# An attention and mixture-of-experts layer: three steps of the attention half in another order

## Chip, cores and metric

The kernel runs on one core of one Trainium2 chip. The metric is the device time of one execution in microseconds (us). The kernel before takes 368.56 us, the median of three runs (367.84 to 369.81).

## What is computed

```python
x = x + attention(layernorm(x), ctx, pos, pos, Wq, Wkv, Wout, bout)   # x: 16 x 128 x 256, ctx: 16 x 128 x 128
x = x + experts(layernorm(x), gate_w, w_gate_up, w_down, ws_gate_up, ws_down)

def attention(x, ctx, pos_map, ctx_pos_map, Wq, Wkv, Wout, bout):     # 32 heads of 8
    q = x @ Wq
    k, v = split(ctx @ Wkv)
    q, k = rope(q, pos_map), rope(k, ctx_pos_map)
    w = softmax(einsum('bqhd,bkhd->bhqk', q, k) / sqrt(8))
    return einsum('bhqk,bkhd->bqhd', w, v) @ Wout + bout
```

The second half routes each token to 6 of 32 experts and adds a shared expert. The change does not touch it. It starts when the attention half has ended, at about 210 us of the span.

## The kernel before

Sixteen batches of 128 tokens pass through a pipeline written out by hand. Every engine has a function `period(b)`, called for b = -3 to 17: the first five calls (`n` from -3 to 1) and the last six (12 to 17) are written out, the ten between them run in a loop of two periods a turn. In the period of batch b the kernel does the scores and exponentials of batch b, begins the row maxima of batch b + 1 (`m1`), transposes the keys of b + 2 (`m2`), projects queries and keys of b + 3 (`m3`), normalises b + 4 (`m4`), and finishes batch b - 1 (`o`). Each period has eight steps g = 0 to 7, one for each group of four heads. An engine takes its instructions strictly in the order written here and waits on semaphores; nothing else sets the order.

On TensorE each step begins with the four score products of batch b, keys by queries (`logits_k`, line 624, into banks STB). In odd steps the row maxima collected so far are transposed (`transpose_max`, line 615). Then comes one product of queries by padded keys, whose rows VectorE reduces to maxima (`logits_q`, line 611, into banks SB). Behind these stand, before the change: in step 0 the value projection of b + 1 (`project_v`, line 601, into bank M0), the transposes of x and context of b + 3 (`transpose_xc`, lines 573 and 574, into M1) and the value products of quads 4 to 7 of batch b - 1 (`weigh_values`, line 635, 32 matmuls); in step 1 the query transposes (`transpose_q`, line 589, into M0) and the key projection (line 578); in step 2 the query projection (line 582); in step 3 the output transposes (line 643); in step 4 the value products of quads 0 to 3 of batch b; in step 5 the attention transposes (line 649); in step 6 the key transposes (`transpose_k`, line 596, into M0); in step 7 the output projection of b - 1 (`project_out`, line 655).

M0 serves in turn the value projection, the query transposes and the key transposes; each must be copied out before the next may write: the values by ScalarE (line 410, semaphore `v_ok`), the queries by ScalarE (line 426), the keys by VectorE (`evac_kT`, line 531, semaphore `kT_ok`). ScalarE also computes the exponentials (line 405, one a step, each also waiting until the value products four steps back have read its buffer), and copies context (line 395, `xcT_ok`), queries and keys (line 416), outputs (`evac_OT`, line 442, after the last value product) and attention (line 420, `attnT_ok`, for which the output projection waits). The value copy of b + 1 waits for all value products of b - 1 as well, since they read the same buffer V. GpSimd rotates and splits queries and keys of b + 3 (lines 264 to 291, tile tokst).

SyncE takes the copied keys kT into the padded tile kz with four transfers a batch (line 319) at the beginning of a period, before it sends the maxima (line 326) in steps 1, 3, 5 and 7. The first product of queries by padded keys, in step 3, waits until all four have landed. kz has two buffers, and the one written was read last by the scores of step 7 of the period before; SyncE therefore waits until all exponentials of that batch are done:

```python
                    else:
                        sp.wait_ge(exp_ok, QUADS * b.n)
```

On its own queue ScalarE issues, in the ten looped periods, the weights of the experts for the second half (352 KB each, after steps 1, 4 and 6).

Of the kernel before, what the change touches and what calls it, by code (L numbers as in the profile page):

```python
# [36 lines left out]
QUADS, SLOT = NH // 4, 32  # L37
# [137 lines left out]
def attention(nc, sem, X, identf, st2, ring, ahead, x, ctx_in, pos, wq, wkv, wout, bout):  # L175
    with ExitStack() as es:
# [119 lines left out]
        @block.sync  # L296
        def _(sp):
            sp.dma_start(POS[:, :, :], pos.rearrange("b p a -> p b a")).then_inc(pos_in, 16)
            for c in range(4):
                sp.dma_start(X[:, 4 * c:4 * c + 4, :], xr[:, 4 * c:4 * c + 4, :]).then_inc(x_in[c], 16)  # L300
                if c == 0:
                    sp.dma_start(CT[0][:, :], ctx_in[0]).then_inc(ctx_in_s[0], 16)
                    sp.dma_start(WQ[:, :, :], wq.rearrange("(c p) n -> p c n", p=P)).then_inc(w_in, 16)
                    sp.dma_start(WKV[:, :], wkv).then_inc(w_in, 16)
                    sp.dma_start(WO[:, :, :], wout.rearrange("(c p) n -> p c n", p=P)).then_inc(w_in, 16)
                    sp.dma_start(BO[:, :], bout.rearrange("(a n) -> a n", a=1).broadcast_to([P, D])).then_inc(bo_in, 16)

            def period(b):
                m1, m4 = b + 1, b + 4
                if inside(m1):  # L310


                    if isinstance(b.n, int) and b.n < 1:
                        sp.wait_ge(kz_zero, 2)
                        sp.wait_ge(kT_ok, m1.n + 1)
                    else:
                        sp.wait_ge(exp_ok, QUADS * b.n)
                    for j in range(4):
                        sp.dma_start(kz[m1.par][32 * j:32 * j + 32, j, :, :],
                                     kT[32 * j:32 * j + 32, :, :]).then_inc(kz_in[m1.par], 16)  # L320
                for g in (1, 3, 5, 7):
                    who, half = (b, (g + 3) // 2) if g < 5 else (m1, (g - 5) // 2)
                    if inside(who):
                        k = 4 * who.n + half
                        sp.wait_ge(mxs_ok, k + 1)
                        sp.dma_start(qst[who.par][MAXROW:P:SLOT, 2 * half:2 * half + 2, :],
                                     mxs[half % 2][:, :]).then_inc(mr_in[half % 2], 16)
                    if g == 1 and inside(m4):
                        at_least(sp, xcT_mm, m4.n - 1)
                        sp.wait_ge(consts, 2)  # L330
                        sp.dma_start(CT[m4.par][:, :], ctx_in[m4.n]).then_inc(ctx_in_s[m4.par], 16)
            periods(sp, period)


# [42 lines left out]
        def _(act):  # L377
# [21 lines left out]
            def period(b):  # L399
                m1, m2, m3, m4, o = b + 1, b + 2, b + 3, b + 4, b + -1  # L400
                for g in range(QUADS):
                    if inside(b):
                        act.wait_ge(st_mm, QUADS * b.n + g + 1)
                        at_least(act, pv_mm, QUADS * b.n + g - 3)
                        act.activation(pw[g % 4][:, :], STB[g % 2][:, :], ACT.Exp, scale=SCALE).then_inc(exp_ok, 1)  # L405
                    if g == 0 and inside(m1):
                        at_least(act, v_mm, m1.n + 1)
                        act.wait_ge(consts, 6)
                        at_least(act, pv_mm, QUADS * b.n)
                        act.copy(Vh[m1.par][:, :, :, 0:HD], M0[:, 0:D].rearrange("p (f h d) -> p f h d", f=2, d=HD)).then_inc(v_ok, 1)  # L410
                    if g == 0 and inside(m3):
                        evac_xcT(m3)
                    if g == 2 and inside(m3) and not (isinstance(b.n, int) and b.n == -3):
                        at_least(act, qk_mm, m3.n + 1)
                        at_least(act, rope_ok, m3.n)
# [1 line left out]
                    if g == 5 and inside(o):  # L417
                        act.wait_ge(attnT_mm, o.n + 1)
                        at_least(act, wo_mm, o.n)
                        act.copy(attnT[:, :, :], OB[o.par][:, D:2 * D].rearrange("p (c t) -> p c t", c=DK)).then_inc(attnT_ok, 1)  # L420
                    if g == 0 and inside(o):
                        evac_OT(o)
                    if g == 1 and inside(m1):
                            at_least(act, qstT_mm, m1.n + 1)
                            at_least(act, st_mm, QUADS * b.n)
# [21 lines left out]
        def _(dve):  # L447
# [85 lines left out]
            def period(b):  # L533
                m1, m2, m3, o, o2 = b + 1, b + 2, b + 3, b + -1, b + -2
                for g in range(QUADS):
# [10 lines left out]
                        statistics2(o2)  # L546
                    if g in (3, 4) and inside(o):
                        normalise(o, g - 3)
                    if g == 6 and inside(m2):
                        evac_kT(m2)  # L550
                    if g == 3 and isinstance(b.n, int) and b.n == -3:
                        dve.wait_ge(qk_mm, 1)
# [10 lines left out]
        def _(pe):  # L563
# [96 lines left out]
            def period(b):  # L660
                m1, m2, m3, o = b + 1, b + 2, b + 3, b + -1
                for g in range(QUADS):
# [6 lines left out]
                    who, u = (b, g + 5) if g < 3 else (m1, g - 3)  # L669
                    if inside(who):  # L670
                        logits_q(who, u)
                    if g == 0 and inside(m1):
                        project_v(m1)
                    if g == 0 and inside(m3):
                        transpose_xc(m3)
                    if g == 0 and inside(o):
                        for q in range(4, QUADS):
                            weigh_values(o, q)
                    if g == 4 and inside(b):
                        for q in range(4):  # L680
                            weigh_values(b, q)
# [7 lines left out]
                        transpose_outputs(o)  # L689
                    if g == 5 and inside(o):  # L690
                        transpose_attn(o)
                    if g == 6 and inside(m2):
                        transpose_k(m2)
                    if g == 7 and inside(o):
                        project_out(o)
            periods(pe, period)


# [708 lines left out]
```

## Time and profile before

| what | value |
|---|---|
| median of 3 runs | 368.56 us |
| profiled execution, its own time | 369.8 us |
| its span | 367.8 us |
| TensorE busy | 315.5 us (86%) |
| VectorE busy | 221.8 us (60%) |
| GpSimd busy | 196.3 us (53%) |
| ScalarE busy | 188.2 us (51%) |

The span runs from the first to the last recorded instruction. PE is TensorE's matmuls, PEld its weight loads, DVE VectorE, ACT ScalarE, POOL GpSimd, SP SyncE. In a timeline each row gives start and length in us, engine, line, operation, what is written and read, how many; rows that follow each other in one group are merged. In brackets stands how long the engine had been idle before, and the instruction by which the profile says it was released. A recorded matmul length holds its way through the array, so successive rows overlap: what a group takes in line is the distance from its start to the next group's start.

### The profile page before, as it was taken

Reading aid. Unit: us, or ns where it says so; the run is one execution under the profiler, and the core shown is the slowest. Engines: PE = TensorE matmul, PEld = TensorE weight load, DVE = VectorE, ACT = ScalarE, POOL = GpSimd, SP = SyncE. Lnnn points to the kernel's source line nnn. Section 1 sums busy time; section 2 is a strip of 40 time slices with the busy share of each in tenths; the row PEclk is TensorE's granted clock in tenths of the full one; section 3 lists DMA queues with packets and bytes.
Section 4 is the critical chain, followed back from the end, with each engine's and each line's share of the span. In section 5 each row is a group of like instructions: output and inputs, shape, how many; then the busy total and the mean of one; then the engine's idle time right before and its main releaser. Section 6 shows DMA issues by size and latency. Waiting matters only on the chain. (4 is left out here: it accounts for less than half of the span.)

```text
span 367.8 us, 9525 instructions
## 1 busy us (share of the span) xinstructions
PE 315.5 (86%) x3094; PEld 218.1 (59%) x3094; DVE 221.8 (60%) x621; ACT 188.2 (51%) x389; POOL 196.3 (53%) x285
## 2 busy tenths in 40 slices
PE   0668999999999999999998558889999989999930
PEld 0445777777777777777676324445765764555520
DVE  4466777676777666777777445788549044454520
ACT  4153668767668767668667375271344342233310
POOL 5569876667866667866200181053788411525460
PEclk9996999999999999999999858999999999999985
DMA  6511114454454454543210033203123275953446
GB/s 169 183 37 30 31 25 116 119 149 118 136 138 115 116 148 115 146 132 87 77 46 3 0 115 111 69 0 87 46 84 105 67 219 181 295 136 44 52 50 228
DMA packets 33292, 37.93 MB, mean 103 GB/s; under 512 B 7808, under 2 KB 27568, under 8 KB 33200
## 3 DMA queue, kind: packets, MB, share of 16 engines
q1 hardware_dynamic: 22610, 22.03, 20.6%
q10 hardware_dynamic: 8030, 11.93, 11.7%
q0 software_dynamic: 2624, 3.61, 5.9%
q8 instruction: 16, 0.26, 0.3%
q14 instruction: 12, 0.10, 0.1%
HBM read 26.36 MB, written 8.96 MB: 96 GB/s over the span
## 5 line engine op out<-in xcount | busy, mean ns | idle before, releaser
L405 ACT ACTIVATE pw<-bank 128x512 f32<-128x512 f32 x128 | 78.0, 615 | 53.3 <-PE bank L635 45.1
L496 DVE TENSOR_REDUCE mx<-bank 128x4 f16<-128x512 f32 x128 | 86.2, 684 | 9.6 <-PE bank L611 8.2
L624 PE MATMUL bank<-qst,kz 128*128 128x128 f16 x512 | 50.3, 221 | 0.3 <-ACT pw L405 0.2
L611 PE MATMUL bank<-kz,qst 128*128 128x512 f16 x128 | 49.6, 389 | 0.9 <-DMA kz<-kT 0.9
L624 PEld LDWEIGHTS bank<-qst,kz 128*128 128x128 f16 x512 | 36.0, 98 | 14.6 <-issue 6.8
L943 POOL DMA_INDIRECT acc<-ac,dst x16 | 23.5, 1471 | 35.3 <-ACT ac L1025 23.4
L264 POOL TENSOR_TENSOR t<-qk,RC 128x512 f32<-128x512 f32 x15 | 19.1, 1272 | 40.2 <-ACT qk L416 40.2
L503 DVE COPY mxs<-bank 8x128 f16<-8x128 f16 x64 | 13.4, 210 | 36.4 <-PE bank L615 36.4
L635 PE MATMUL bank<-pw,V 128*32 128x128 f32 x1024 | 34.6, 276 | 0.0
L1245 PE MATMUL mbank<-hT,WSG 128*128 128x512 f16 (+1 forms) x144 | 32.0, 379 | 0.0
L635 PEld LDWEIGHTS bank<-pw,V 128*32 128x32 f32 x1024 | 26.0, 109 | 7.3 <-issue 5.0
L899 POOL TENSOR_TENSOR ac<-ac,sg 128x512 f32<-128x512 f32 (+1 forms) x9 | 11.8, 1323 | 25.7 <-ACT ac L979 25.7
L269 POOL TENSOR_TENSOR t<-qk,RS 128x256 f32<-128x256 f32 x30 | 24.7, 844 | 0.0
L1245 PEld LDWEIGHTS mbank<-hT,WSG 128*128 128x128 f16 (+1 forms) x144 | 15.0, 106 | 15.6 <-ACT ac L979 0.4
L1257 PE MATMUL mbank<-WSD,ac 128*128 128x256 f32 (+1 forms) x96 | 21.7, 382 | 1.9 <-POOL ac L899 1.9
L289 POOL TENSOR_TENSOR tokst<-rot,tokst 128x256 f16<-128x256 f32 x30 | 20.1, 672 | 4.4
L278 POOL TENSOR_TENSOR rot<-t 128x256 f32<-128x256 f32 x30 | 21.1, 726 | 2.1 <-POOL t L269 1.7
L1257 PEld LDWEIGHTS mbank<-WSD,ac 128*128 128x128 f32 (+1 forms) x96 | 17.9, 189 | 5.4 <-POOL ac L899 2.9
L1029 ACT ACTIVATE ac<-mbank 128x176 f32<-128x176 f32 x16 | 5.1, 317 | 29.9 <-PE mbank L1335 29.9
L615 PE MATMUL bank<-identh,mx 128*128 128x128 f16 x64 | 14.4, 225 | 6.8 <-DVE mx L496 5.2
L1335 PE MATMUL mbank<-ring_gu,xbT 128*64 128x352 f32 x112 | 19.1, 461 | 0.7 <-ACT xbT L819 0.7
L582 PE MATMUL bank<-WQ,xcT 128*128 128x256 f32 x64 | 18.2, 411 | 0.0
(192 smaller groups left out, 640.2 us busy)
## 6 DMA issues: line engine op xcount, KB each, us to landing
ring_gu<-in_L_ffn_w_gate_up ACTq DMA_DIRECT2D x20, 352.0 KB
kz<-kT SPq DMA_DIRECT2D x64, 64.0 KB, 2.0
ring_dn<-in_L_ffn_w_down ACTq DMA_DIRECT2D x10, 352.0 KB
ring_gu<-in_L_ffn_w_gate_up SPq DMA_DIRECT2D x8, 352.0 KB
X<-in_x SPq DMA_DIRECT2D x4, 512.0 KB, 8.1
table<-ac SPq DMA_DIRECT2D x8, 256.0 KB, 2.2
acc<-X SPq DMA_DIRECT2D x4, 512.0 KB, 3.7
out<-acc SPq DMA_DIRECT2D x4, 512.0 KB, 5.6
```

The lines of the kernel that those rows point to most:

```text
L264: eng.tensor_tensor(o1, source[:, :].rearrange("p (x a) -> p x a", a=8), rc, ALU.mult)
L269: ins = eng.tensor_tensor(o2[:, :, :, r], pairs[:, :, :, 1 - r], rs, ALU.mult)
L278: eng.tensor_tensor(rot[:, part], t1[:, part], t2[:, part], ALU.add).then_inc(rot_ok[w], 1)
L289: eng.tensor_tensor(tokst[m.par][:, w, :, a:a + HD], r, hi, ALU.subtract)
L405: act.activation(pw[g % 4][:, :], STB[g % 2][:, :], ACT.Exp, scale=SCALE).then_inc(exp_ok, 1)
L496: dve.tensor_reduce(mx[u // 2 % 2][:, u % 2:8:2], SB[u % 2][:, :].rearrange("p (j t) -> p j t", j=4), axis=AX.X, op=ALU.max, negate=True). ...
L611: pe.matmul(SB[u % 2][:, :], qst[m.par][:, u, :], kz[m.par][:, :, u, :], start=True, stop=True).then_inc(s_mm, 1)
L624: ins = pe.matmul(STB[g % 2][:, j * P:j * P + P], kz[m.par][:, j, g, :], qst[m.par][:, g, :], start=True, stop=True)
L635: ins = pe.matmul(OB[m.par][32 * j:32 * j + 32, (g % 4) * P:(g % 4) * P + P], V[m.par][:, a:a + SLOT], pw[g % 4][:, j * P:j * P + P], star ...
L943: pool.indirect_dma_start(acc[:, :], bass.IndirectOffsetOnAxis(ap=dst[0:USED, k:k + 1], axis=0), ys[j][0:USED, :], None, compute_op=ALU.ad ...
L1245: ins = pe.matmul(GU[2 * (i % 2) + w][0:n, :], WSG[:, c, u, w * SHARED + a:w * SHARED + a + n], hT[:, v, c, 512 * k:512 * k + 512], start= ...
L1257: ins = pe.matmul(DN[m % 2][:, 0:D], ac[k % 2][0:n, f, j * P:j * P + P], WSD[0:n, f, :], start=(f == 0), stop=(f == 2))
```

## The change

The order of four engines is rewritten, and one wait is exchanged. No instruction is added or removed.

- Step 0 on TensorE: value products of b - 1 first, then the x and context transposes, then the value projection. ScalarE follows: output copy, context copy, value copy.
- Step 6 on TensorE: the output projection. Step 7: the key transposes. VectorE's key copy moves from step 6 to step 7.
- SyncE's padded-key transfers wait for the key copy (`kT_ok`) in all periods, as they did in the first ones. The copy comes after the key transposes, and these now stand behind the step-7 scores, the last readers of the kz buffer.

```diff
--- before.py
+++ after.py
@@ -314,7 +314,7 @@
                         sp.wait_ge(kz_zero, 2)
                         sp.wait_ge(kT_ok, m1.n + 1)
                     else:
-                        sp.wait_ge(exp_ok, QUADS * b.n)
+                        sp.wait_ge(kT_ok, m1.n + 1)
                     for j in range(4):
                         sp.dma_start(kz[m1.par][32 * j:32 * j + 32, j, :, :],
                                      kT[32 * j:32 * j + 32, :, :]).then_inc(kz_in[m1.par], 16)
@@ -403,13 +403,15 @@
                         act.wait_ge(st_mm, QUADS * b.n + g + 1)
                         at_least(act, pv_mm, QUADS * b.n + g - 3)
                         act.activation(pw[g % 4][:, :], STB[g % 2][:, :], ACT.Exp, scale=SCALE).then_inc(exp_ok, 1)
+                    if g == 0 and inside(o):
+                        evac_OT(o)
+                    if g == 0 and inside(m3):
+                        evac_xcT(m3)
                     if g == 0 and inside(m1):
                         at_least(act, v_mm, m1.n + 1)
                         act.wait_ge(consts, 6)
                         at_least(act, pv_mm, QUADS * b.n)
                         act.copy(Vh[m1.par][:, :, :, 0:HD], M0[:, 0:D].rearrange("p (f h d) -> p f h d", f=2, d=HD)).then_inc(v_ok, 1)
-                    if g == 0 and inside(m3):
-                        evac_xcT(m3)
                     if g == 2 and inside(m3) and not (isinstance(b.n, int) and b.n == -3):
                         at_least(act, qk_mm, m3.n + 1)
                         at_least(act, rope_ok, m3.n)
@@ -418,8 +420,6 @@
                         act.wait_ge(attnT_mm, o.n + 1)
                         at_least(act, wo_mm, o.n)
                         act.copy(attnT[:, :, :], OB[o.par][:, D:2 * D].rearrange("p (c t) -> p c t", c=DK)).then_inc(attnT_ok, 1)
-                    if g == 0 and inside(o):
-                        evac_OT(o)
                     if g == 1 and inside(m1):
                             at_least(act, qstT_mm, m1.n + 1)
                             at_least(act, st_mm, QUADS * b.n)
@@ -546,7 +546,7 @@
                         statistics2(o2)
                     if g in (3, 4) and inside(o):
                         normalise(o, g - 3)
-                    if g == 6 and inside(m2):
+                    if g == 7 and inside(m2):
                         evac_kT(m2)
                     if g == 3 and isinstance(b.n, int) and b.n == -3:
                         dve.wait_ge(qk_mm, 1)
@@ -669,13 +669,13 @@
                     who, u = (b, g + 5) if g < 3 else (m1, g - 3)
                     if inside(who):
                         logits_q(who, u)
-                    if g == 0 and inside(m1):
-                        project_v(m1)
-                    if g == 0 and inside(m3):
-                        transpose_xc(m3)
                     if g == 0 and inside(o):
                         for q in range(4, QUADS):
                             weigh_values(o, q)
+                    if g == 0 and inside(m3):
+                        transpose_xc(m3)
+                    if g == 0 and inside(m1):
+                        project_v(m1)
                     if g == 4 and inside(b):
                         for q in range(4):
                             weigh_values(b, q)
@@ -689,10 +689,10 @@
                         transpose_outputs(o)
                     if g == 5 and inside(o):
                         transpose_attn(o)
-                    if g == 6 and inside(m2):
+                    if g == 6 and inside(o):
+                        project_out(o)
+                    if g == 7 and inside(m2):
                         transpose_k(m2)
-                    if g == 7 and inside(o):
-                        project_out(o)
             periods(pe, period)
 
 
```

TensorE, steps 6 and 7 and the start of the next step 0, in the period of batch 12. L624 are scores, L611 queries by padded keys, L596 key transposes, L615 the maxima's transpose, L655 the output projection. Before:

```order
L611 MATMUL bank<-kz,qst 128x512
L596 MATMUL bank<-identh,tokst 128x128 x8
L624 MATMUL bank<-qst,kz 128x128 x4
L615 MATMUL bank<-identh,mx 128x128
L611 MATMUL bank<-kz,qst 128x512
L655 MATMUL bank<-WO,attnT 128x256 x2
L624 MATMUL bank<-qst,kz 128x128 x4
```

And now:

```order
L611 MATMUL bank<-kz,qst 128x512
L655 MATMUL bank<-WO,attnT 128x256 x2
L624 MATMUL bank<-qst,kz 128x128 x4
L615 MATMUL bank<-identh,mx 128x128
L611 MATMUL bank<-kz,qst 128x512
L596 MATMUL bank<-identh,tokst 128x128 x8
L624 MATMUL bank<-qst,kz 128x128 x4
```

The projection and the key transposes have changed places around the scores and the maxima's transpose of step 7.

ScalarE, from the last exponential of one period to the query copy (L426) of the next, in the period of batch 1. L410 is the value copy (L414 in the changed file), L395 the context copy, L442 the output copy, L405 an exponential. Before:

```order
L405 ACTIVATE pw<-bank 128x512 x4
L410 COPY V<-bank 128x2x16x8
L395 COPY xcT<-bank 128x384
L442 COPY OT<-bank 128x512
L405 ACTIVATE pw<-bank 128x512
L426 COPY qst<-bank 128x1024
```

And now:

```order
L405 ACTIVATE pw<-bank 128x512 x4
L442 COPY OT<-bank 128x512
L395 COPY xcT<-bank 128x384
L414 COPY V<-bank 128x2x16x8
L405 ACTIVATE pw<-bank 128x512
L426 COPY qst<-bank 128x1024
```

The value copy now comes last of the three copies, the output copy first.

## Rows read from the trace of the kernel before

**Rows 1.** Timeline of TensorE, period of batch 7: start, length, line, operation

```profile
108.59 0.39 PE L624 MATMUL bank<-qst,kz 128*128 128x128 f16 x4
...
109.03 0.59 PE L601 MATMUL bank<-WKV,xcT 128*128 128x256 f32 x2
109.46 0.38 PE L573 MATMUL bank<-identf,xn 128*128 128x128 f32 x2
...
109.88 1.08 PE L635 MATMUL bank<-pw,V 128*32 128x128 f32 x32
...
111.18 0.38 PE L611 MATMUL bank<-kz,qst 128*128 128x512 f16 x1
...
114.13 0.38 PE L611 MATMUL bank<-kz,qst 128*128 128x512 f16 x1
...
115.32 1.08 PE L635 MATMUL bank<-pw,V 128*32 128x128 f32 x32
...
117.49 0.61 PE L596 MATMUL bank<-identh,tokst 128*128 128x128 f16 x8
117.94 0.39 PE L624 MATMUL bank<-qst,kz 128*128 128x128 f16 x4
...
118.75 1.03 PE L655 MATMUL bank<-WO,attnT 128*128 128x256 f32 x4
...
119.62 0.39 PE L624 MATMUL bank<-qst,kz 128*128 128x128 f16 x4
```

**Rows 2.** Timeline of ScalarE, the same period

```profile
111.10 0.37 ACT L410 COPY V<-bank 128x256 f32<-128x256 f32 x1
111.37 0.48 ACT L395 COPY xcT<-bank 128x384 f32<-128x384 f32 x1
111.74 0.60 ACT L442 COPY OT<-bank 128x512 f32<-128x512 f32 x1
...
117.33 0.37 ACT L420 COPY attnT<-bank 128x256 f32<-128x256 f32 x1
```

**Rows 3.** Timelines of weight loads (PEld) and ScalarE, same period and batch 14's

```profile
111.59 0.46 PEld L589 LDWEIGHTS bank<-identh,tokst 128*128 128x128 f16 x8 [0.36 <-POOL tokst L291]
...
118.44 0.10 PEld L615 LDWEIGHTS bank<-identh,mx 128*128 128x128 f16 x1 [0.29 <-DVE mx L496]
...
187.21 0.37 ACT L410 COPY V<-bank 128x256 f32<-128x256 f32 x1
...
187.69 0.46 PEld L589 LDWEIGHTS bank<-identh,tokst 128*128 128x128 f16 x8 [0.36 <-issue]
```

**Rows 4.** Timeline of all engines, last output projection of the attention half

```profile
207.19 0.37 ACT L420 COPY attnT<-bank 128x256 f32<-128x256 f32 x1 [2.17 <-PE bank L649]
...
207.61 1.13 PE L655 MATMUL bank<-WO,attnT 128*128 128x256 f32 x4 [0.46 <-ACT attnT L420]
```

**Rows 5.** Timeline of TensorE in batch -1's period, then windows table with granted clock

```profile
30.29 1.06 PE L596 MATMUL bank<-identh,tokst 128*128 128x128 f16 x8
...
31.32 0.10 PEld L615 LDWEIGHTS bank<-identh,mx 128*128 128x128 f16 x1 [0.24 <-DVE mx L496]
...
core 0: us, PE busy (x) PEld busy (x) DVE busy (x) ACT busy (x) POOL busy (x), PEclk, DMA share, GB/s
...
30.00:32.00 2.00, 2.00 (x13) 1.29 (x13) 1.88 (x4) 0.00 (x0) 1.92 (x4) 0.50 0.01 1
```

**Rows 6.** Timeline of weight loads and TensorE, periods of batches 14 and 16

```profile
193.97 0.10 PEld L615 LDWEIGHTS bank<-identh,mx 128*128 128x128 f16 x1 [0.74 <-DVE mx L496]
...
203.29 1.08 PE L635 MATMUL bank<-pw,V 128*32 128x128 f32 x32
```

**Rows 7.** Timelines of VectorE, SyncE and TensorE, then landings of line 319's transfers

```profile
118.30 0.68 DVE L531 COPY kT<-bank 128x1024 f16<-128x1024 f16 x1
...
21.83 2.53 SPq L319 DMA_DIRECT2D kz<-kT  x4
...
25.93 0.59 PE L611 MATMUL bank<-kz,qst 128*128 128x512 f16 x2 [0.91 <-DMA kz<-kT]
...
DMA to landing us min/median/max: 2.0/2.0/3.1
```

## The prediction

> **What bounds the kernel now.** The change touches only the attention half, so I read that half by period. TensorE's timeline first: from the first score product of one batch (step 0, at 108.59 us) to that of the next (119.62) is 11.03 us [rows 1], and the matmuls stand almost shoulder to shoulder. TensorE sets the pace; the other engines cost time only where it waits for them. I call the period's start E and the start of its step-4 value products (115.32, E + 6.73) W. The next period starts at W + 4.30.
>
> Then TensorE's weight loads, for the holes. Two come back in each period. At step 7 the transpose of the maxima waits for the last row maximum: 0.29 us [rows 3]. At step 1 the query transposes (line 589) start their load at 111.59. In line, 0.22 after the score product at 111.18 [rows 1], they would start at 111.40, so 0.2 us is lost. The profile names GpSimd's key and query split as the releaser. The rows speak against it: ScalarE's copy of the values started 0.49 earlier, at 111.10 [rows 2], and at 187.69, where GpSimd is not named, the load again stands 0.48 behind a value copy [rows 3]. Both products use bank M0, so the transposes wait for that copy. The two holes, 0.5 us a period, are all that a new order can win.
>
> **The change, part by part** (the sum is against the profiled execution's own 369.8 us; the median of the runs shown, 368.56, lies 1.2 below, and I move the sum onto it).
>
> *Step 0, value products first.* The 32 value products take 1.01 (109.88 to 110.89 by their place in line), the context and x transposes 0.42, the value projection 0.43 [rows 1]. Their sum is unchanged, so TensorE reaches the query transposes at the same E + 2.81. What matters is when the value copy runs, since it now stands behind the output copy and the context copy on ScalarE. Before, it started 1.22 after the start of the products [rows 1, 2]. Now the products start at E + 0.44, so the output copy starts by E + 1.66. ScalarE's next instruction starts about 0.11 before the recorded end of the one before (V 0.37 long, next start 0.27 later [rows 2]): output copy 0.49, context copy 0.37, value copy at E + 2.52. The value projection, at E + 1.87 and 0.59 long, ends at E + 2.46, just in time. The copy started at E + 2.51 before. The hole stays; bounds -0.2 (if it vanished) and +0.1 (if the late projection holds the copy back); I take +0.02. The earlier exponential of step 0 frees nobody, since its products are due only in step 4.
>
> *Steps 6 and 7, output projection against key transposes.* The projection (0.87 in line, 118.75 to 119.62) now stands where the transposes stood (117.49, W + 2.17; they take 0.45) [rows 1]. It needs the attention copy, which starts at 117.33, W + 2.01 [rows 2]. Where the projection was seen waiting for this copy it started 0.42 after the copy's start, at 207.61, and the group was 1.13 long instead of 1.03 [rows 4, 1]: its load is not hidden. So it starts at W + 2.43 and the step-7 scores at W + 3.30 (load free) or W + 3.40 (load 0.10 in the open). The maxima's transpose is due 0.22 later (117.94 to 118.44 is 0.50, less the hole of 0.29 [rows 1, 3]), at W + 3.51 to 3.61; the maximum lets it go at W + 3.12, so this hole is gone. Behind it 0.31 (118.44 to 118.75) and the key transposes 0.45: the period ends at W + 4.27 to 4.37, against 4.30. **One hole is traded for another**: -0.03 to +0.07. I take +0.07, by the row that shows a waiting projection.
>
> The Trainium skill ("TensorE: Matmul & The Clock Gate", Part 2, "Step-by-step: what each phase is for") says that the array pulls weight loads ahead of matmuls in flight, so that they overlap. By that the load would be free and the term -0.03. Here the operand loaded is the awaited copy itself, and the trace with its 1.13 disagrees. No other number rests on this.
>
> With +0.02 from step 0 this is +0.09 for each of the twelve periods of batches 1 to 12, which hold all moved pieces: **+1.1** (bounds -0.1 and +2.0; with the hole at step 1 gone, -2.5).
>
> *Fill.* In the period of batch -1 the clock is granted at half, 1.2 GHz (0.50 in 30 to 32 us), and the key transposes at 30.29, 1.06 long, lie wholly inside a wait of the maxima's transpose, which ends at 31.32 [rows 5]. In step 7 they lie in the open before batch 0's first scores: 0.85 at this clock, of which about half is won back where the work behind it runs after the rise to full speed. Bounds 0.4 and 0.85: +0.6. In batch 0's period there is no output projection to put in their old place: they leave the shadow of the step-7 hole and add up to their 0.45 [rows 1]; I take +0.4. Together **+1.0**.
>
> *Drain.* In batch 13's period nothing changes in kind. In batch 14's there are no key transposes; the step-7 hole is 0.74 [rows 6], and the projection moved in front of it fills it, less its own wait of about 0.2 and the open load of 0.1: -0.45. In batch 15's the projection stands between the step-7 scores and the last value products, which start at 203.29 [rows 6]. In front of the scores it delays them by its own 0.97 and the 0.2 of its wait, 1.2; three of the four groups of value products (0.25 each) need not wait for the last exponential, and the end moves by about +0.45 (bounds 0 and 1.2). Nothing covers this: copy, transposes and last projection follow one another to the next half. Together **0**.
>
> *The transfers.* The padded keys' four issues waited for the exponentials of the batch before, now for the key copy. Key transposes, 0.61 long, start at W + 3.92; with a maximum of 0.69 in VectorE's way the copy (0.68 [rows 7]) ends by about E + 1.1. From the first issue to the first product that waited for them was 4.10 us (21.83 to 25.93 [rows 7]), so they are there at E + 5.2. They are needed at 114.13, E + 5.54 [rows 1]. Nothing is late as long as a landing stays near 2.0 us; 3.1 us is the longest seen [rows 7]. Behind these issues SyncE has the maxima's transfer of step 1, some 0.4 later than before, wanted only in step 6. VectorE gets the key copy ahead of the x update and one maximum, 0.68 later; that maximum is wanted at E + 2.5 and ready by about E + 2.1. Cost: nothing, with 0.3 us of cover in the first case and 0.4 in the second.
>
> Sum: 1.1 + 1.0 + 0 = +2.1 us, so 371.9 for the profiled execution and **370.7** for the median.
>
> **The rivals.** *No measurable difference (369.4).* The projection's load is hidden after all: -0.03 a period instead of +0.07, the twelve give 0 with the term of step 0, and 1.0 of fill would give 369.6; with the low bound of the fill 369.2; I write 369.4. For it: the terms are small and half the fill is a guess about the clock. Against: the row of 1.13. By the page named above this would be the case.
>
> *Faster (366.1).* The step-7 hole goes and the projection does not wait. The mechanism: ScalarE, relieved in step 0, has the attention copy done by W + 2.17 instead of W + 2.38. Then -0.29 for each of twelve periods, -3.5, and with +1.0 of fill 366.1. It decides at a copy start 0.2 us earlier. Against: that copy follows an exponential that value products of step 4 release, which moves with W, and not with step 0. If the hole at step 1 goes as well, another -2.5 gives 363.6.
>
> *Slower by more (373).* Under the ring's transfers the last of the padded keys lands up to 1.1 us later than 2.0, against 0.3 of cover: up to 0.8 a period. At 0.2 on average over twelve periods, +2.4 on the forecast: 373.1. It decides at a landing above 2.3 us. For it: the longest is 3.1. Against: issues are now about 1 us later, when the weight transfers of step 6 should be over.
>
> **How the numbers follow.** A measurement of this kernel can tell about 0.5%, 1.8 us, from no change, so faster means under 366.7 and slower above 370.4. My forecast of 370.7 gets 0.40, no difference 0.35, faster 0.13, late transfers 0.12. The forecast lies so near the bound that a quarter of its weight falls below it. Slower: three quarters of 0.40 and the 0.12, 0.42. Same: 0.35 and the other quarter, 0.45. Faster 0.13. The range leaves out the deeper half of the faster case and the far end of late transfers: 367.0 to 373.2.
>
> **What would show it.** Right: a period of 11.05 to 11.15 us; the maxima's transpose of step 7 without a wait; line 655's load waiting 0.2 to 0.3 for the attention copy, its group 1.13 long; the query transposes still 0.48 behind the value copy; ScalarE's long idle before step 0's exponential shorter by 0.85; batch 0's first scores up to 0.85 later. Wrong: a period under 11.0, a wait of the step-3 scores for the padded keys, or query transposes that start in line.

## The result, and the profile after

| | before | after |
|---|---|---|
| median of 4 runs | 368.76 us (367.84 to 369.81) | 382.22 us (378.45 to 383.08) |
| profiled execution, its own time | 369.8 us | 381.86 us |
| its span | 367.8 us | 379.8 us |
| first output transposes (line 643) | 48.09 us | 49.07 us |
| end of the attention half (line 1206) | 210.0 us | 220.92 us |
| TensorE busy | 315.5 us | 320.3 us |

The changed kernel takes 1.033 times as long, 95% interval 1.028 to 1.038. Here and below a time is the median of all runs, while ratios and intervals are formed from each kernel's fast runs, those within 1.5% of its fastest, which leaves out half of the runs of experiments 5 and 8, in experiment 6 one run of 645 us, and beside 9 and 10 one run of the kernel before of 1083 us. The prediction was 370.7 us with a range to 373.2: the side was right, the size far off.

The 12.0 us between the two spans can be placed with the start times of line 643 (step 3 of each period). **Fill**: +0.98 up to the first. **The eleven distances from there to batch 12's period**: 127.82 against 121.42, +6.40. Nine of them alternate between 11.52 and 11.57 where 11.03 stood; the first is 11.68 (11.09 before), the second 12.22. **Drain**, the last four and the way to the end of attention: 10.51, 12.07, 10.24, 6.30 against 10.27, 10.09, 9.24, 5.97, +3.55. **Second half**, which the change does not touch: +1.1.

TensorE's timeline of batch 7's period, now from 112.96 (E) to 124.47:

```profile
112.96 0.39 PE L624 MATMUL bank<-qst,kz 128*128 128x128 f16 x4
...
113.49 1.08 PE L635 MATMUL bank<-pw,V 128*32 128x128 f32 x32
114.50 0.44 PE L573 MATMUL bank<-identf,xn 128*128 128x128 f32 x2
114.78 0.27 PE L574 MATMUL bank<-identf,CT 128*128 128x128 f32 x1
114.89 0.60 PE L601 MATMUL bank<-WKV,xcT 128*128 128x256 f32 x2
...
116.42 0.61 PE L589 MATMUL bank<-identh,tokst 128*128 128x128 f16 x8 [0.44 <-ACT V L414]
...
120.12 1.08 PE L635 MATMUL bank<-pw,V 128*32 128x128 f32 x32
...
122.56 1.13 PE L655 MATMUL bank<-WO,attnT 128*128 128x256 f32 x4
123.53 0.39 PE L624 MATMUL bank<-qst,kz 128*128 128x128 f16 x4
123.75 0.22 PE L615 MATMUL bank<-identh,mx 128*128 128x128 f16 x1
123.81 0.38 PE L611 MATMUL bank<-kz,qst 128*128 128x512 f16 x1
124.02 0.61 PE L596 MATMUL bank<-identh,tokst 128*128 128x128 f16 x8
124.47 0.39 PE L624 MATMUL bank<-qst,kz 128*128 128x128 f16 x4
```

ScalarE and the weight loads of the same period:

```profile
114.64 0.58 ACT L442 COPY OT<-bank 128x512 f32<-128x512 f32 x1
115.52 0.48 ACT L395 COPY xcT<-bank 128x384 f32<-128x384 f32 x1 [0.30 <-PE bank L601]
115.89 0.38 ACT L414 COPY V<-bank 128x256 f32<-128x256 f32 x1
...
116.39 0.46 PEld L589 LDWEIGHTS bank<-identh,tokst 128*128 128x128 f16 x8 [0.74 <-POOL tokst L291]
...
122.56 0.73 PEld L655 LDWEIGHTS bank<-WO,attnT 128*128 128x128 f32 x4 [0.43 <-ACT attnT L422]
```

E is the start of the period and W that of its step-4 value products, as in the prediction. Read against [rows 1 to 3]: from E to the step-4 value products it is 7.16 us, where 6.73 stood; from these to the next E 4.35, where 4.30 stood. The loss lies in the first part. The idle time before the query transposes' load has grown from 0.36 to 0.74, and their distance behind E from 3.03 to 3.46. ScalarE's rows above show why: the context copy (L395) starts at 115.52, just behind the end of the value projection (114.89 + 0.60), and in brackets it names that projection. The value copy queued behind it starts at E + 2.93.

In the second part the load of L655 waits 0.43 in step 6, and L615 has no wait any more.

In the drain, the period of batch 14. TensorE's timeline, then line 319's landings and the windows table with the granted clock (PEclk):

```profile
197.26 0.23 PE L615 MATMUL bank<-identh,mx 128*128 128x128 f16 x1 [0.56 <-DVE mx L496]
199.10 0.58 PE L611 MATMUL bank<-kz,qst 128*128 128x512 f16 x1 [1.60 <-issue]
199.47 1.06 PE L643 MATMUL bank<-identf,OT 128*128 128x128 f32 x4
```

```profile
L319 SPq DMA_DIRECT2D kz<-kT x4: 558/588/592, 193.7 to 195.6; - x4
...
DMA to landing us min/median/max: 2.0/2.2/3.4
```

```profile
core 0: us, PE busy (x) PEld busy (x) DVE busy (x) ACT busy (x) POOL busy (x), PEclk, DMA share, GB/s
195.00:198.00 3.00, 1.87 (x22) 1.14 (x19) 2.14 (x5) 2.71 (x5) 0.00 (x0) 1.00 0.36 86
198.00:201.00 3.00, 1.90 (x10) 1.47 (x10) 1.05 (x2) 0.07 (x1) 0.00 (x0) 0.65 0.02 5
201.00:204.00 3.00, 3.00 (x46) 2.12 (x45) 1.73 (x4) 1.37 (x4) 0.00 (x0) 0.78 0.00 0
```

The first product of queries by padded keys started 0.10 behind L615 in this period of the kernel before (189.56, 189.66); here it starts 1.84 behind it, with TensorE idle for 1.60. The last of the four transfers was issued at 195.6 and the slowest landing took 3.4, which gives 199.0. From the first issue (193.70) to the product's place in line (197.36) there are 3.7 us here; in batch 7's period it is 4.9 (issue at 114.03, product at 118.93), since steps 0 to 2 there also hold the x and context transposes and the key and query projections of a batch to come, and the last periods have none of these. Behind this pause and the 0.56 ahead of it the granted clock falls to 0.65, a mix of TensorE's two levels (0.5 is 1.2 GHz): the output transposes take 1.06 where 0.60 is their length at 2.4 GHz.

The odd distance of 12.22, batch 2's period, is a third matter. SyncE's and TensorE's timelines:

```profile
55.46 3.52 SPq L319 DMA_DIRECT2D kz<-kT  x4
59.12 0.58 SPq L326 DMA_DIRECT2D qst<-mxs  x1
...
61.87 0.40 PE L624 MATMUL bank<-qst,kz 128*128 128x128 f16 x4 [0.52 <-DMA qst<-mxs]
```

The four issues took 3.52 instead of 2.46. The maxima's transfer stands behind them in SyncE's queue, 0.9 later than in the other periods, and the scores of step 4 wait for it until 2.75 behind its issue. In the same period ScalarE issued its first weight transfer at 58.73, 0.39 ahead of the maxima's (in batch 7's period it comes 0.64 behind). Experiments 4 and 5 are about such meetings.

### The profile page after: what moved, and what is told of

The parts are those of the page before. It is cut to its first block and busy times, and to the rows that moved or that the text cites. A ratio compares the mean times of both kernels' runs of the same rounds, so it can differ in the third digit from the quotient of the medians.

```text
span 379.8 us, 9525 instructions
## 1 busy us (share of the span) xinstructions
PE 320.3 (84%) x3094; PEld 217.2 (57%) x3094; DVE 222.6 (59%) x621; ACT 192.0 (51%) x389; POOL 196.3 (52%) x285
## 5 line engine op out<-in xcount | busy, mean ns | idle before, releaser
L405 ACT ACTIVATE pw<-bank 128x512 f32<-128x512 f32 x128 | 76.7, 603 | 50.9 <-PE bank L635 30.3
L611 PE MATMUL bank<-kz,qst 128*128 128x512 f16 x128 | 49.8, 391 | 2.2 <-issue 1.8
L624 PE MATMUL bank<-qst,kz 128*128 128x128 f16 x512 | 50.4, 222 | 0.9 <-DMA qst<-mxs 0.5
L624 PEld LDWEIGHTS bank<-qst,kz 128*128 128x128 f16 x512 | 37.5, 99 | 14.6 <-issue 3.4
L1335 PE MATMUL mbank<-ring_gu,xbT 128*64 128x352 f32 x112 | 20.5, 488 | 0.7 <-ACT xbT L819 0.7
L655 PE MATMUL bank<-WO,attnT 128*128 128x256 f32 x64 | 18.1, 405 | 2.2 <-ACT attnT L422 1.0
```

What stands on the lines that cost most here:

```text
L611: pe.matmul(SB[u % 2][:, :], qst[m.par][:, u, :], kz[m.par][:, :, u, :], start=True, stop=True).then_inc(s_mm, 1)
L624: ins = pe.matmul(STB[g % 2][:, j * P:j * P + P], kz[m.par][:, j, g, :], qst[m.par][:, g, :], start=True, stop=True)
L1335: ins = pe.matmul(EB[k % 2][lane, 0:2 * INNER], xbT[:, c, e * CAP:e * CAP + LANE], ring.gu[place][:, e % 2, c, :], start=(c == 0), stop=(c ...
```

## The experiments

All changes are in step 0 unless a diff shows more. A kernel's time stands beside runs of the kernel before on the same chip. A period's length is read as a distance between starts of line 643.

**1. The change, with ScalarE's value copy ahead of the context copy.**

```diff
                         evac_OT(o)
-                    if g == 0 and inside(m3):
-                        evac_xcT(m3)
                     if g == 0 and inside(m1):
...
                         act.copy(Vh[m1.par][:, :, :, 0:HD], M0[:, 0:D].rearrange("p (f h d) -> p f h d", f=2, d=HD)).then_inc(v_ok, 1)
+                    if g == 0 and inside(m3):
+                        evac_xcT(m3)
```

> The changed kernel with one difference on ScalarE: in step 0 the value copy stands before the context copy (output, value, context). Theory 1 (the context copy waits for the value projection, by its guard on v_mm, and holds the value copy behind it): the value copy starts right behind the projection's end, 0.34 earlier, the query transposes 0.4 earlier, periods 11.1 instead of 11.54, about 5 us less: 377. Theory 2 (the late value projection itself holds the value copy, so its place among the copies does not matter): no change, 382.

Measured: 376.68 us beside 369.09, ratio 1.020 (1.011 to 1.029). ScalarE's and TensorE's timelines, batch 7's step 0 and 1:

```profile
114.46 0.37 ACT L412 COPY V<-bank 128x256 f32<-128x256 f32 x1 [0.30 <-PE bank L601]
114.73 0.48 ACT L395 COPY xcT<-bank 128x384 f32<-128x384 f32 x1
...
114.98 0.60 PE L589 MATMUL bank<-identh,tokst 128*128 128x128 f16 x8
```

From batch 4's period on the period is 11.13: 0.41 of the 0.51 is gone with two instructions of ScalarE exchanged. So the context copy's wait made it. What is left, +0.10 over the 11.03 of before, is what the prediction had (+0.09). The two periods ahead of these are longer, 11.97 and 12.05: in each the scores of step 4 wait for the maxima, 0.66 and 0.70 us, and the first weight transfer is issued 0.42 and 0.05 ahead of the maxima's. Batch 14's pause is there too (1.13).

**2. The kernel before with the change's step 0 alone.** Against the changed kernel:

```diff
-                        sp.wait_ge(kT_ok, m1.n + 1)
+                        sp.wait_ge(exp_ok, QUADS * b.n)
...
-                    if g == 7 and inside(m2):
+                    if g == 6 and inside(m2):
                         evac_kT(m2)
...
-                    if g == 6 and inside(o):
-                        project_out(o)
-                    if g == 7 and inside(m2):
+                    if g == 6 and inside(m2):
                         transpose_k(m2)
+                    if g == 7 and inside(o):
+                        project_out(o)
```

> The kernel before with the change's step 0 alone (value products first, value projection last, output copy first on ScalarE); steps 6 and 7 and the transfers' wait as before. Theory 1: period 11.03 + 0.43 = 11.47, 12 to 13 periods, about 374.5. Theory of the prediction (step 0 costs 0.02 a period): 369. If the loss comes from steps 6 and 7 instead: no slower than 369.

Measured: 375.51 us, ratio 1.018 (1.010 to 1.026). Periods 11.46 and 11.51 in turn, +0.46, and no product of any of them waits for a transfer; the drain is as before (10.19, 10.19, 9.23, 5.96), with no late transfer. Its period is 0.06 shorter than the whole change's: that is the size of steps 6 and 7.

**3. The whole change, but step 0 in the old order on TensorE and ScalarE.** TensorE's part, ScalarE's copies likewise:

```diff
+                    if g == 0 and inside(m1):
+                        project_v(m1)
+                    if g == 0 and inside(m3):
+                        transpose_xc(m3)
                     if g == 0 and inside(o):
...
-                    if g == 0 and inside(m3):
-                        transpose_xc(m3)
-                    if g == 0 and inside(m1):
-                        project_v(m1)
```

> The changed kernel with step 0 in its old order on TensorE and ScalarE; output projection in step 6, key transposes in step 7 and the new wait stay. The value projection at the head of step 0 must now wait for the key copy, which ends at E + 1.07: it starts at E + 1.1 instead of 0.44, and its hole of 0.67 is added to 0.07 of the waiting output projection: period 11.75, about 378. Rival (the two halves are independent and step 0 carries all of the loss): 370.

Measured: 383.69 us, ratio 1.039 (1.030 to 1.048), worse than expected. TensorE's timeline:

```profile
116.31 0.70 PE L601 MATMUL bank<-WKV,xcT 128*128 128x256 f32 x2 [0.49 <-DVE kT L531]
```

The value projection at the head of step 0 writes bank M0, which holds the keys until VectorE has copied them; with the key transposes in step 7 it waits 0.49 for that copy, and with its load in the open takes 0.10 longer. The period is 11.85 (batch 3's 12.52, where the scores of step 4 wait 0.50 for the maxima). So the change's two halves belong together: key transposes in step 7 need a step 0 that leaves M0 alone at first.

**4. The change, with the value projection between value products and transposes** (copies: output, values, context). Meant to take away the hole of step 1 altogether.

```diff
                         for q in range(4, QUADS):
                             weigh_values(o, q)
-                    if g == 0 and inside(m3):
-                        transpose_xc(m3)
                     if g == 0 and inside(m1):
                         project_v(m1)
+                    if g == 0 and inside(m3):
+                        transpose_xc(m3)
```

> The changed kernel with the value projection between the value products and the x and context transposes, and the copies in that order (output, value, context). Theory 1: value copy at E + 2.17, query transposes in line at E + 2.8, so the hole of step 1 is gone too: period 11.54 - 0.65 = 10.9, about 374 (the fill, the late keys of batch 14 and the output projection's wait stay). Theory 2: the hole of the kernel before, 0.2, stays: period 11.1, 377.

Measured: 382.19 us, ratio 1.035 (1.027 to 1.043): a miss. The query transposes do follow in line, yet the looped periods are 11.55 to 11.88 from batch 3's on. SyncE's, ScalarE's and TensorE's timelines show a new wait:

```profile
118.53 0.58 SPq L326 DMA_DIRECT2D qst<-mxs  x1
...
118.61 0.39 ACTq L122 DMA_DIRECT2D ring_gu<-in_L_ffn_w_gate_up  x1
...
121.80 0.40 PE L624 MATMUL bank<-qst,kz 128*128 128x128 f16 x4 [0.68 <-DMA qst<-mxs]
```

The maxima of 2 KB are waited for until 3.27 us behind their issue. A weight transfer of 352 KB is issued 0.08 behind them. One further product waited 2.34 for padded keys in an early period, and batch 14's again came late (12.39).

**5. The same, with the first weight transfer issued after step 2 instead of step 1.**

```diff
-                    if g in (1, 4, 6) and not isinstance(b.n, int):
-                        ring.load_first(act, b.n - 2, (1, 4, 6).index(g))
+                    if g in (2, 4, 6) and not isinstance(b.n, int):
+                        ring.load_first(act, b.n - 2, (2, 4, 6).index(g))
```

> The kernel v_second (382) with the first of ScalarE's three weight transfers of a period issued after step 2 instead of step 1. Theory 3: in v_second the maxima's transfer of step 1 is issued at 118.53 on SyncE, in line behind the four padded-key issues, and the 352 KB weight transfer at 118.61 shares the 16 engines with it; its landing takes 3.3 us and step 4 waits 0.7. With the weights 1.3 later it lands in about 2 us: no wait of the step-4 scores, period 10.9, about 372 to 374. Rival (SyncE's late issue alone is the cause, and 3.3 us is what such a small transfer takes): no change, 382.

Measured: 374.16 us in 10 runs beside 369.81 in 25, ratio 1.006 (0.999 to 1.013). Idle time of TensorE's products that the maxima's transfer ended, in the view of waits, of experiment 4 and then of this one (us in total, times, longest):

```profile
PE bank L624 <- DMA qst<-mxs: 5.5, 9, 0.8
```

```profile
PE bank L624 <- DMA qst<-mxs: 1.1, 4, 0.4
```

The periods are 11.14 on average. All nine waits of step 4 are gone, with one issue of another queue moved: the collision of the two transfers is shown. It was not removed but moved. The four waits left are those of the scores of step 6, for the maxima that are sent in step 3, and the weight transfer now stands just ahead of these (batch 6's period: weights issued at 104.95, maxima at 105.20). The ratio went from 1.035 to 1.006, by the medians of all runs to 1.012. Not all of that is this waiting: experiment 4 also lost 2.34 us once to padded keys (0.78 here) and 1.1 us more behind batch 14's pause (distance 10.02 against 8.91). In batch 14's period the padded keys still come late (landing at most 3.1 us, period 11.56).

**6. Experiment 1 with the old order of steps 6 and 7, and the old wait, from batch 12's period on.**

```diff
+                    elif isinstance(b.n, int) and b.n > 12:
+                        sp.wait_ge(exp_ok, QUADS * b.n)
...
-                    if g == 6 and inside(o):
+                    last = isinstance(b.n, int) and b.n >= 12
+                    if g == (7 if last else 6) and inside(o):
                         project_out(o)
```

Key transposes and key copy go back to step 6 in these periods in the same way.

> The kernel act_v_second (376.7) with the old order of steps 6 and 7 and the old wait in the written-out last periods (batch 12 on). Theory 4 (in the short last periods the padded keys, issued 1 us later, have no cover, and the wait of 1 to 1.6 us also drops the clock): no wait in step 3 of batch 14's period and no half clock after it; in batch 15's period the scores of step 7 are early again (-0.4). Together -1.5 to -3: 374 to 375. Rival (that late landing is chance or not tied to the order): the wait stays, 376 to 377.

Measured: 375.81 us, ratio 1.015 (1.004 to 1.026) where experiment 1 had 1.020; the intervals overlap, so the verdict rests on the trace. TensorE's timeline at the place of the 1.60, step 3 of batch 14's period (all lines stand two further down):

```profile
191.42 0.23 PE L617 MATMUL bank<-identh,mx 128*128 128x128 f16 x1 [0.56 <-DVE mx L498]
191.52 0.38 PE L613 MATMUL bank<-kz,qst 128*128 128x512 f16 x1
191.73 0.60 PE L645 MATMUL bank<-identf,OT 128*128 128x128 f32 x4
```

No product of this period waits for padded keys, and none runs at half clock. The transfers, issued from 186.89 on, are 4.6 us ahead of the product instead of 3.7, and all four landed within 2.0: they have their cover back.

**7. The kernel before with step 0 in the order of experiment 4** (steps 6 and 7 untouched).

> The kernel before with step 0 as value products, value projection, transposes of x and context, and the copies output, value, context; steps 6 and 7 and the transfers' wait as before. Theory 1: the value copy starts at E + 2.2 and the query transposes stand in line, so the hole of 0.22 at step 1 goes, and neither the output projection waits nor are the padded keys or the maxima late: period 10.82, 13 periods, about 366. Rival (the hole is GpSimd's, as the profile names it, or the maxima's transfer of step 4 comes late here too): 368.5 or more.

Measured: 369.69 us in 10 runs, ratio 0.997 (0.992 to 1.001). The periods are 10.90 to 10.91, 0.13 less than before: the hole of step 1 was real, but worth 0.13 and not 0.2. That is 1.5 us over eleven distances, about what the measurement can tell; its interval holds 1, so no gain is claimed. The profiled 364.48 us comes mostly from an earlier fill (first line 643 at 44.08 instead of 48.09).

**8. Experiment 7 with the output projection in step 7 moved ahead of the maxima's transpose**, to fill its hole with no swap of steps.

```diff
+                    if g == 7 and inside(o):
+                        project_out(o)
...
-                    if g == 7 and inside(o):
-                        project_out(o)
```

> The kernel f_vsecond with the output projection in step 7 moved from behind the products of that step to between the scores and the maxima's transpose, so that it fills the wait for the last maximum. The attention copy ends 0.4 before it. The hole of 0.29 goes; the copy of the maxima comes 0.6 later and the product of step 0 that overwrites its bank may wait 0.1 to 0.15 for it: period 10.82 - 0.15 to 0.29, about 363 to 364.5. Rival (the later copy and transfer of the maxima cost as much): 366 or more.

Measured: 370.64 us, ratio 0.996 (0.991 to 1.001). Every second period reaches 10.7; the others are 11.35 to 11.66, with this in the timelines of SyncE, ScalarE and TensorE:

```profile
102.52 0.59 SPq L326 DMA_DIRECT2D qst<-mxs  x1
...
102.47 0.39 ACTq L122 DMA_DIRECT2D ring_gu<-in_L_ffn_w_gate_up  x1
...
105.75 0.40 PE L624 MATMUL bank<-qst,kz 128*128 128x128 f16 x4 [0.77 <-DMA qst<-mxs]
```

**9 and 10. Experiments 7 and 8 with the weight transfer after step 2** (diff of experiment 5).

> The kernel before with step 0 in the order value products, value projection, context transposes (ScalarE's copies: output, values, context), and the first weight transfer of a period issued after step 2 instead of after step 1. The order of step 0 alone gave periods of 10.90 us and no wait for the maxima, so there is nothing left for the later weight transfer to repair: theory (the weight transfer hurts only where it meets the maxima's transfer) expects the same 10.90 and the time of f_vsecond, ratio to before 0.994 to 0.998. Rival: a weight transfer issued 1.3 us later collides with the padded keys' transfer that starts behind step 7, and the step-3 scores wait: slower than before by 1 to 3 us.

> g_outfirst (output projection in front of the maxima's transpose) with the first weight transfer issued after step 2. If the wait of the step-4 score maxima for their transfer (0.50 to 0.77 us in every other period) comes from the weight transfer that starts beside it, it goes: all periods at 10.7 us, 12 x 0.33 = 4 us less than the kernel before, ratio 0.987 to 0.992. Rival: the maxima's transfer is late because its maximum is, whatever else moves: periods still alternate and the ratio stays at 0.996.

Measured: 371.82 us, ratio 1.004 (1.001 to 1.007), and 369.81 us, ratio 1.001 (0.997 to 1.005), beside 370.13. Both miss: in 9 the time is the rival's, but not for its reason, since no product of the looped periods waits for padded keys. The distances are 10.9 to 11.5 in 9 and 11.06 on average in 10 (without its first, 11.82, in which a product waited 0.97 for padded keys). ScalarE, SyncE and TensorE in 9, batch 7's period:

```profile
113.73 0.59 ACT L418 COPY qk<-bank 128x512 f32<-128x512 f32 x1 [0.27 <-PE bank L582]
113.90 0.39 ACTq L122 DMA_DIRECT2D ring_gu<-in_L_ffn_w_gate_up  x1
114.24 5.56 SPq L326 DMA_DIRECT2D qst<-mxs  x3
114.45 0.60 ACT L405 ACTIVATE pw<-bank 128x512 f32<-128x512 f32 x1
115.55 0.60 ACT L405 ACTIVATE pw<-bank 128x512 f32<-128x512 f32 x1 [0.49 <-PE bank L635]
...
116.51 0.38 PE L649 MATMUL bank<-identf,attn 128*128 128x128 f32 x2
116.53 0.59 ACT L405 ACTIVATE pw<-bank 128x512 f32<-128x512 f32 x1
...
117.20 0.38 PE L624 MATMUL bank<-qst,kz 128*128 128x128 f16 x4 [0.31 <-ACT pw L405]
```

The scores of step 6 start 0.69 behind the attention transposes (L649), where 7 has 0.21 (111.99 and 112.20). In brackets the profile names an exponential, the one of step 5 that starts at 116.53. The program does not wait for that one:

```python
                at_least(pe, exp_ok, QUADS * m.n + g - 1)
```

With g = 6 these are the exponentials of steps 0 to 4, and the one of step 4 ended at 116.15. The scores' other wait is for the maxima sent in step 3. Their transfer was issued at 114.24, 0.34 behind the moved weight transfer, so it is this wait, until 2.96 behind the issue; in 7 the scores start 2.48 behind it and do not wait. Over the ten looped periods the scores of step 6 come 4.03 us later in all than they do in 7, and the ten periods are 4.05 longer in all. The issue on ScalarE also puts off the exponential of step 3, which starts 0.72 behind the copy's start instead of 0.48; by the rows no product waits for it. In 10 the five waits of step 4 that 8 had (2.9 us) are gone, and the scores of step 6 are late in nine of the ten periods, by 3.6 us in all. So the later weight transfer left one transfer of maxima alone and met the next. No order of the ten was measurably faster than the kernel before.

## Why the prediction was wrong, point by point

**The step that failed: "output copy 0.49, context copy 0.37, value copy at E + 2.52".** I let the copies follow each other without asking what each waits for. The context copy of b + 3 writes the buffer from which the value projection of b + 1 still reads (they share `m3.par`), and waits for it: `at_least(act, v_mm, m.n - 1)`. Before, the projection was the first thing in step 0 and the wait was always met. At the end of step 0 it is the last thing to be met, and the value copy stands behind the waiting copy. It starts at E + 2.93, 0.41 later than I had it. Experiment 1 removes the coupling: the value copy starts at E + 2.56, and the period is +0.10 against the predicted +0.09. The term of step 0 was +0.02 and my upper bound for it +0.1; it measured +0.46 (experiment 2), 5 us of the 12.

**Steps 6 and 7: right.** The projection waits for the attention copy (its load at W + 2.44, predicted W + 2.43), is 1.13 long, the maxima's transpose has no wait, and the period's second part is 0.05 longer (predicted 0.07; experiment 2 gives 0.06). The load was in the open again. What the Trainium skill says of weight loads ("TensorE: Matmul & The Clock Gate", Part 2, "Step-by-step: what each phase is for"), that they are pulled ahead of matmuls in flight, did not help here, where the operand loaded is the one waited for. The reading of the hole in step 1 was right too: it follows the value copy, and GpSimd, which the profile still names, has no part in it. Its worth of 0.2 was too high (0.13, experiment 7). That the two parts can be added up one by one, as I did, holds only because step 0 changed as well: experiment 3 has steps 6 and 7 alone at +0.82.

**Fill: +1.0 predicted, +0.98 read, by luck.** A single trace cannot tell this term. Experiments 1 and 6 have the same order up to batch 12's period, and their first line 643 stands at 49.00 and 46.64. The direction is borne out: from the first product of queries by padded keys to batch 0's first scores it is 5.90 before and 6.74 after, 0.84 more where I had up to 0.85, and 6.11 to 7.11 in all kernels with the key transposes in step 7 there against 5.25 to 6.13 in the others. It fits that in the periods of batches -1 and 0 the maximum of step 7 still keeps its transpose waiting (0.83 and 0.49), with the key transposes behind it in the open. Its size stays open.

**Drain: the terms held, a transfer was missing.** In experiments 1 and 5, the last two distances are 8.91 and 6.29 against 9.24 and 5.97: -0.33 and +0.32, where I had -0.45 and +0.45. What broke the sum is the sentence "They are needed at 114.13, E + 5.54": I took the looped period for all. Step 0 of batch 14's period still has the value projection, but no x and context transposes, and steps 1 and 2 have no key and query projections; the key copy has moved behind step 7, and nothing of the cover of 0.3 is left. With a landing of 3.4 it cost 1.60 and the clock behind it, 1.3 more by the distance of 10.24 instead of 8.91. Experiment 6 shows that the order and wait of steps 6 and 7 cause it. Why the longest landing was 3.0 to 3.8 in this period of the changed kernel and of experiments 1, 4 and 5, and 2.0 in all the others, stays open.

**The transfers.** The padded keys were issued at E + 1.07 (predicted 1.1) and were not late in the looped periods. But "the maxima's transfer of step 1 ... wanted only in step 6" was wrong: the scores of step 4 wait for it. It cost 0.52 once in the changed kernel and 1.4 in two periods of experiment 1, and in experiments 4 and 8 it decided the result. The rival "slower by more" named the padded keys and a price per period; the keys were late at one place, where the pipeline drains.

**The second half's +1.1** was in no step, and the other traces do not tie it to the change. The weight products of line 1335 average 488 ns there, where they averaged 461 before. They average 488 in experiments 1, 2, 6 and 9 too, and 461 in 3, 4, 5, 7, 8 and 10, so kernels with changed steps 6 and 7 stand on both sides, and so do kernels with a changed step 0. From its first matmul to the end of the span the half takes 156.5 to 160.5 us in the ten.

Together: 6.4 in the eleven distances (5.1 by step 0, 0.7 by steps 6 and 7, 0.6 by the maxima, 12.22 against 11.57), 1.0 fill, 3.55 drain, 1.1 second half: 12.0.

## What to carry to other kernels

When instructions are put in another order, write out every wait of every instruction that moves and of those that now stand behind it, the guards of double buffers too, and ask of each when it is met in the new order; a guard that was always met long ago is the one that is overlooked. Look at cover in the shortest period of a pipeline, not in the loop. In experiments 4, 5, 8, 9 and 10 a gain of a few tenths a period was paid back by a small transfer that came to stand next to a large one, so read the issue times of all queues before moving anything, and again at the place where it goes. Where an instruction has two waits, look up in the program which of them the named instruction can have released.

## What the runs showed of the hardware

- A small transfer is slowed by a large one issued close to it from another engine. The 2 KB of maxima were waited for until 3.27 us behind their issue where 352 KB were issued 0.08 later (experiment 4), and 3.23 where these came 0.05 earlier (8). With the large issue up to 0.58 ahead, the wait lasted until 2.75 to 2.9 behind the small one's (changed kernel and experiments 1 and 8, batch 2's period). With it 0.21 to 0.26 behind (changed kernel, batch 3's period, and experiment 1 from batch 4's on), scores due 2.6 behind the issue did not wait; nor did they with 0.49 (7) or 0.64 (changed kernel, batch 7's), where they were due 2.9 and 3.0 behind it. With the large issue 0.25 to 0.35 ahead (9 and 10, step 3's maxima), scores due 2.5 behind the small one's waited until 2.7 to 3.1.
- The issue of a transfer on ScalarE's queue, 0.39 long, put off the exponential behind it by 0.24 us, although it overlaps the copy ahead of it (experiment 9).
- Pauses of 0.56 and 1.60 us in one stretch were followed by a granted clock of 0.65 (changed kernel), of 0.56 and 1.91 by 0.52 (experiment 4), and of 0.56 and 1.13 (1) or 0.56 and 1.25 (5) by 1.00. Batch 14's pause in the changed kernel cost nearly as much again in clock as in waiting.
- Four equal issues of 64 KB took 2.45 us in nearly all periods and 3.52 in batch 2's. No run tells why.
